# One layer stack on one core: value products paired every eight slots, two copies of x moved in SyncE's queue, eight first max scores moved into the first phase

## The chip, the cores and the metric

The kernel runs on one core of a Trainium2 chip. A core has a matrix engine (TensorE, PE in the rows, with its weight loads as PEld), a vector engine (VectorE, DVE), a scalar engine (ScalarE, ACT), GpSimd (POOL), and SyncE (SP), which here only issues DMAs. The engines have queues of their own, run in the order in which the program was written for each, and meet at semaphores. The metric is the device time of one execution in microseconds (us). The kernel before took 1245.22 us in the median of three runs (1243.57 to 1249.75).

## The reference, cut to what matters

```python
# x: 8 sequences of 512 tokens, 256 wide; 16 heads of 16
def attention_a(x):                       # plain: every query sees every key
    q, k, v = heads(x @ qkv_w.T + qkv_b)
    p = softmax(q @ k.T / sqrt(16))
    return (p @ v) @ out_w.T + out_b
def attention_b(x):                       # causal, with rotary positions
    q, k = rotate(heads(x @ Wq.T)), rotate(heads(x @ Wk.T))
    p = softmax(where(causal, q @ k.T / sqrt(16), -1e9))
    return (p @ v) @ Wo.T
def ffn(x):                               # soft tree of depth 8: 255 gates, 256 leaves
    gate = sigmoid((x @ Wq.T) @ routers.T)
    return (leaf_products(gate) @ leaf_values) @ Wout_w.T + Wout_b
x = x + attention_a(layernorm(x)); x = x + ffn(layernorm(x))
x = x + attention_b(layernorm(x)); x = x + ffn(layernorm(x))
```

## The kernel before

**Phases and slots.** Eight sequences with two attentions each make 16 phases. `causal(n)` says which are causal: phases 3, 5, 7, 9, 11, and 13 to 15. One phase is the attention of one sequence (16 heads, 512 queries, 512 keys), cut into 64 slots. Four slots make a step: a group `g` of four heads against one block `kb` of 128 keys. In a slot TensorE issues:

- one score matmul (line 1068, `ps_max<-k_stack,q_stack`) into one of three PSUM banks `ps_max`. VectorE takes the largest score of each query from it (lines 829 and 825, 825 in a causal phase). This runs `LEAD` = 28 slots ahead, so from slot 36 on it works for the next phase. I call it S below.
- one keyed matmul (line 1090, `ps_key<-q_stack,k_stack`): the same scores with the keys on the rows, already less the largest score, into one of two banks `ps_key`. ScalarE turns it into `probs` (line 737, the exp). I call it K.

**Value products.** `mixed` (line 1114, `ps_out<-probs,v_ones`) multiplies the four `probs` of a step with the values: four matmuls of 32 columns of weights each, side by side in TensorE's four column tiles, all other matmuls of the kernel being one over all 128 columns. In the trace each is two instructions, so a step is a row of x8. `MIX_LAG` = 8 puts step s at slot 4s + 8, so there is one at every slot that is a multiple of four. In a causal phase block kb covers only 512, 384, 256 or 128 queries.

**The largest scores' way.** After 16 score units VectorE turns `neg_max` (line 840), SyncE sends it by four DMAs into a row of `q_stack` (line 471), and the K of that head group waits for them. In the opening 28 units run before slot 0, and the first send follows the unit of slot -10.

**The other work** sits in the same slots by hand-written tables (`FINISH`, `PREPARE_PLAIN`, `PREPARE_CAUSAL`, `LATE`): output projection, layernorm (lines 924 to 954), gates (1197), the tree's levels (976 to 985) and mixing of the phase before, and heads (1222), rotation and the bf16 parts of q and k of the next. For a causal next phase `high_q`, `middle_q` and `low_q` come at slots 20, 22 and 23. SyncE then copies each part into `q_stack` by DMAs (`stack`, line 495): six for the high part, four for the middle one, two for the low one. S at slot 36 is the first to need them all, since it is unit 0 of the next phase.

**Copies of x.** x lives in several tiles; `keep` copies `x_moved` to `x_kept` (line 558), `move` copies `x_plain` to `x_moved` (line 548). `move` waits until the `keep` before it has landed. In phases 4, 6, 8, 10 and 12 both are issued by SyncE with `project_out` 1 of the phase before, at slot 23, and that table entry sorts ahead of `low_q` 1 in the same slot. The line that a sentence can't say is the sum that decides which value products stand in a slot:

```python
if slot % GROUP == MIX_LAG % GROUP:
    step = (slot - MIX_LAG) // GROUP
```

## Time and profile before

| | |
|---|---|
| median of three runs | 1245.22 us (1243.57 to 1249.75) |
| the profiled execution's own time | 1240.59 us |
| its span | 1238.8 us |
| PE / PEld busy | 1113.4 us (90%) / 545.2 us (44%) |
| DVE / ACT / POOL busy | 927.5 us (75%) / 720.7 us (58%) / 302.8 us (24%) |
| opening, up to the first K | 54.7 us |
| a causal phase (5) / a plain one (6) | 65.8 us / 78.0 us |
| after the last K | about 33 us |

A row gives the start, the length, the engine, the line, the operation, output<-inputs, and a count where rows were merged. Idle time ahead of it stands in brackets with what ended it. Matmuls are pipelined: the next one starts before the row of the last has ended, so what one costs is read from start to start.

### The profile page before, as it was taken

How to read it: one execution, taken by the hardware profiler on the slowest of the kernel's cores; microseconds unless marked ns; L12 is line 12 of the kernel's file. 1: busy time of each engine (PE TensorE's matmuls, PEld its weight loads, DVE VectorE, ACT ScalarE, POOL GpSimd, SP SyncE). 2: the span in 40 equal slices, each digit the busy share in tenths (PEclk: the TensorE clock that was granted, in tenths of full speed). 3: DMA queues.
4: the chain of work that ended last, by engine and by line, in shares of the span. 5: the costliest groups of instructions: out<-in, count | busy, mean ns of one | idle time of the engine just before them, and what ended most of it. 6: DMA issues, size and time to landing. Idle time of an engine off the chain costs nothing.

```text
span 1238.8 us, 18868 instructions
## 1 busy us (share of the span) xinstructions
PE 1113.4 (90%) x6160; PEld 545.2 (44%) x6160; DVE 927.5 (75%) x2599; ACT 720.7 (58%) x1457; POOL 302.8 (24%) x324
## 2 busy tenths in 40 slices
PE   5789999879998999989999898989999898887986
PEld 3133443434544554434544354434544444443544
DVE  3768788767878779867889669777888668875834
ACT  3166755557556675657657574656757566554551
POOL 3011101312223031411324022320315125252210
PEclk9599999989999999999999999999999899998988
DMA  7231401122204050230404141041402203011000
GB/s 211 57 96 42 103 18 35 52 69 83 55 18 136 18 120 2 65 106 18 103 1 127 45 97 24 22 133 33 106 1 66 89 18 103 2 49 55 19 3 32
DMA packets 67122, 75.33 MB, mean 61 GB/s; under 512 B 12465, under 2 KB 52817, under 8 KB 67025
## 3 DMA queue, kind: packets, MB, share of 16 engines
q1 hardware_dynamic: 66960, 74.09, 22.3%
q8 instruction: 50, 0.82, 0.3%
q14 instruction: 48, 0.39, 0.1%
q0 software_dynamic: 64, 0.03, 0.0%
HBM read 12.45 MB, written 4.19 MB: 13 GB/s over the span
## 4 chain that ended last, share of the span: by engine, by line
PE 52%; DVE 24%; SPq 6%; DMA 6%; ACT 5%; issue 4%; POOL 2%; DVEq 0%; ACTq 0%; POOLq 0%
PE ps_work L1197 12%; PE ps_out L1114 11%; PE ps_max L1068 9%; PE ps_key L1090 9%; PE ps_work L1222 8%; DVE neg_max L829 6%; SPq L495 4%; DVE ps_max L825 4%; DMA q_stack<-q_part 3%; DVE scratch L982 3%; ACT probs L737 2%; PE ps_work L1168 2%; DVE scratch L954 2%; DVE scratch L985 2%; DMA x_kept<-x_moved 2%
## 5 line engine op out<-in xcount | busy, mean ns | idle before, releaser
L737 ACT ACTIVATE probs<-ps_key 128x512 f32<-128x512 f32 (+3 forms) x1024 | 514.9, 519 | 440.2 <-PE ps_key L1090 436.3
L1068 PE MATMUL ps_max<-k_stack,q_stack 96*128 96x512 bf16 (+3 forms) x1024 | 359.5, 354 | 75.9 <-DMA q_stack<-q_part 44.8
L829 DVE TENSOR_REDUCE neg_max<-ps_max 128x1 bf16<-128x512 f32 x512 | 336.6, 683 | 88.0 <-PE ps_max L1068 86.7
L1090 PE MATMUL ps_key<-q_stack,k_stack 97*128 97x512 bf16 (+3 forms) x1024 | 353.6, 348 | 15.4 <-ACT probs L737 12.7
L825 DVE CUSTOM_DVE_ANT_0 ps_max<-ps_max,mask_b 128x128 f32<-128x128 f32 (+3 forms) x512 | 247.8, 502 | 151.1 <-PE ps_max L1068 149.6
L1068 PEld LDWEIGHTS ps_max<-k_stack,q_stack 96*128 96x128 bf16 x1024 | 99.8, 98 | 348.9 <-DVE neg_max L829 120.1
L1114 PE MATMUL ps_out<-probs,v_ones 128*32 128x512 f32 (+3 forms) x2048 | 238.7, 539 | 0.6 <-POOL probs L642 0.6
L642 POOL TENSOR_SCALAR_AFFINE_SELECT probs<-probs 128x512 f32<-128x512 f32 x128 | 83.0, 648 | 457.6 <-ACT probs L737 457.0
L1090 PEld LDWEIGHTS ps_key<-q_stack,k_stack 97*128 97x128 bf16 x1024 | 101.3, 99 | 136.6 <-ACT probs L737 85.2
L664 POOL TENSOR_TENSOR rstd<-variance,minus_half 128x4 f32<-128x4 f32 (+1 forms) x34 | 33.2, 976 | 235.9 <-DVE variance L937 204.9
L1168 PE MATMUL ps_work<-ident,scratch 128*128 128x128 f32 x384 | 64.2, 293 | 21.6 <-DMA a_v_bias<-in_a_v_bias 9.3
L1197 PE MATMUL ps_work<-gate_w,turned_block 128*128 128x255 f32 x256 | 73.2, 414 | 1.4 <-ACT turned_block L758 1.4
L1114 PEld LDWEIGHTS ps_out<-probs,v_ones 128*32 128x32 f32 x2048 | 40.6, 109 | 74.6 <-issue 66.8
L825 DVE DVE_READ_ACCUMULATOR2_ANT neg_max<- 128x1 bf16 x512 | 73.0, 143 | 0.0
L1168 PEld LDWEIGHTS ps_work<-ident,scratch 128*128 128x128 f32 x384 | 47.4, 149 | 46.6 <-DVE scratch L954 24.1
L1197 PE MATMUL ps_work<-leaf_w,turned_block 128*128 128x256 f32 x256 | 66.3, 383 | 1.4 <-ACT turned_block L758 1.4
L758 ACT ACTIVATE turned_block<-ps_work 128x512 f32<-128x512 f32 x96 | 57.3, 598 | 12.6 <-PE ps_work L1168 12.4
L684 POOL TENSOR_TENSOR scratch<-scratch,cosine 128x512 f32<-128x512 f32 x32 | 43.5, 1358 | 66.8 <-ACT scratch L773 35.7
L1197 PEld LDWEIGHTS ps_work<-gate_w,turned_block 128*128 128x128 f32 x256 | 53.4, 213 | 12.6 <-ACT turned_block L758 2.0
L704 POOL TENSOR_TENSOR k_part<-scratch,k_part 128x512 bf16<-128x512 f32 x32 | 40.3, 1271 | 67.7 <-ACT k_part L795 67.7
L1197 PEld LDWEIGHTS ps_work<-leaf_w,turned_block 128*128 128x128 f32 x256 | 46.0, 190 | 11.6 <-ACT turned_block L758 1.9
L704 POOL TENSOR_TENSOR q_part<-scratch,q_part 128x512 bf16<-128x512 f32 x32 | 38.0, 1191 | 40.5 <-ACT q_part L795 40.4
(83 smaller groups left out, 1201.0 us busy)
## 6 DMA issues: line engine op xcount, KB each, us to landing
k_stack<-k_part SPq DMA_DIRECT2D x48, 256.0 KB
q_stack<-q_part SPq DMA_DIRECT2D x48, 256.0 KB
k_stack<-k_part SPq DMA_DIRECT2D x96, 128.0 KB
q_stack<-q_part SPq DMA_DIRECT2D x96, 128.0 KB
x_in<-in_x SPq DMA_DIRECT2D x8, 512.0 KB, 4.1
q_stack<-shift_rows SPq DMA_DIRECT2D x256, 1.0 KB, 1.7
x_again<-in_x SPq DMA_DIRECT2D x8, 512.0 KB, 4.0
x_moved<-x_plain SPq DMA_DIRECT2D x7, 512.0 KB, 3.5
```

Source lines behind the costliest of these rows:

```text
L642: pool.affine_select(out=tile, in_=tile, compare_op=ALU.is_ge, fill=0.0, base=0, pattern=[[0, GROUP], [1, P]], channel_multiplier=-1)\
L704: pool.tensor_tensor(parts[which][2][:, i, :], rest_of(which, m)[:, i, :], parts[which][1][:, i, :], ALU.subtract).then_inc(on["low"], 1)
L737: act.activation(probs[step % RING][:, j, q0:T], ps_key[slot % 2][:, 0:T - q0], ACT.Exp, scale=SCALE).then_inc(on["exp_done"], 1)
L758: act.activation(dst[:, :, 2 * P * i:2 * P * i + 2 * P], bank[:, :].rearrange("p (k n) -> p k n", k=KC), ACT.Copy).then_inc(on["turned"], 1)
L825: dve.tensor_tensor_reduce(out=src, in0=src, in1=mask_b[:, T - keys:], scale=-1.0, scalar=-MASKED, op0=ALU.add, op1=ALU.min, accum_out=dst)\
L829: dve.tensor_reduce(out=dst, in_=src, axis=AX_X, op=ALU.max, negate=True)\
L1068: pe.matmul(dst[:, 0:keys], q_stack[n % 2][0:SPLIT_ROWS, h, P * qt:P * qt + P], k_stack[n % 2][0:SPLIT_ROWS, h, 0:keys], start=True, stop= ...
L1090: pe.matmul(ps_key[slot % 2][:, 0:T - q0], k_stack[n % 2][0:STACK_ROWS, h, P * kb:P * kb + P], q_stack[n % 2][0:STACK_ROWS, h, q0:T], star ...
L1114: last = pe.matmul(ps_out[COLS * j:COLS * j + COLS, q0:T], v_flat[n % 2][:, at:at + COLS], probs[step % RING][:, j, q0:T], start=(kb == 0) ...
L1168: last = pe.transpose(by_tile(bank)[:, k, P * t:P * t + P], src[:, 2 * i + t, P * k:P * k + P], ident[:, :])
L1197: last = pe.matmul(by_tile(bank)[:, t, 0:width], turned[:, k, tile], weight[:, k, 0:width], start=(k == 0), stop=(k == KC - 1))
L1222: last = pe.matmul(bank[:, :], weight[:, k, P * i:P * i + P], turned_heads[:, k, :], start=(k == 0), stop=(k == KC - 1))
```

## The change

Three things move; none is added or dropped.

1. `mixed` runs for two steps in a row at slots 4, 12, 20, ..., 60, and no more at slots 0, 8, 16, ..., 56. The later step of each pair stands where it stood, the earlier one four slots later than before. Pairs are of steps (14, 15) of the phase before at slot 4, then (0, 1), (2, 3) and so on; 127 pairs in all, and the last two steps stay in the closing.
2. `keep` and `move` leave `project_out` 1 and go to slots 24 and 31 of the same five phases, behind the stack DMAs of `low_q`.
3. The opening runs 20 score units, not 28; in slots 0 to 7 of phase 0 two units run in each slot.

```diff
+CATCH_UP = 8
+KEEP_SLOT, MOVE_SLOT = 24, 31
+def lead_slots(n, slot):
+
+    if n == 0 and slot < CATCH_UP:
+        return 2 * slot - CATCH_UP, 2 * slot - CATCH_UP + 1
+    return slot,
...
+            def core(n, slot):
+                for at in lead_slots(n, slot):
+                    send_shift(n, at)
...
+                if 0 < n < PHASES - AHEAD and causal(n - 1):
+                    if slot == KEEP_SLOT:
+                        keep()
+                    if slot == MOVE_SLOT:
+                        move()
+
             def project_out(m, i, n, bank):
                 count.add("x_ready")
-                if i == 1 and causal(m) and n < PHASES - AHEAD:
-                    keep()
-                    move()
...
             def opening():
-                for slot in range(-LEAD, 0):
+                for slot in range(-LEAD, -CATCH_UP):
                     send_shift(0, slot)
...
             def core(n, slot):
-                largest(n, slot)
+                for at in lead_slots(n, slot):
+                    largest(n, at)
...
             def core(n, slot):
-                ahead(n, slot)
+                for at in lead_slots(n, slot):
+                    ahead(n, at)
                 if out_due(n, slot) is not None:
-                    turn_out(out_due(n, slot), 1, bank_of["turn_out", n, slot])
+                    turn_out(out_due(n, slot), 0, bank_of["turn_out", n, slot])
                 by_key(n, slot)
-                if slot % GROUP == MIX_LAG % GROUP:
-                    step = (slot - MIX_LAG) // GROUP
-                    if step >= 0:
-                        mixed(n, step, MIX_LAG - GROUP + 1)
-                    elif n > 0:
-                        mixed(n - 1, step + STEPS, MIX_LAG - GROUP + 1)
+                if slot % (2 * GROUP) == (MIX_LAG + GROUP) % (2 * GROUP):
+                    step = (slot - MIX_LAG) // GROUP - 1
+                    for late in range(2):
+                        if step >= 0:
+                            mixed(n, step + late, MIX_LAG - GROUP + 1)
+                        elif n > 0:
+                            mixed(n - 1, step + late + STEPS, MIX_LAG - GROUP + 1)
```

TensorE in phase 6, from S of slot 16 to S of slot 21, before. L1068 is S, L1090 is K, L1114 a step's value products (x4 in the program), L1197 a half of the output projection:

```order
L1068 MATMUL ps_max<-k_stack,q_stack 128x512
L1090 MATMUL ps_key<-q_stack,k_stack 128x512
L1114 MATMUL ps_out<-probs,v_ones 32x512 x4
L1068 MATMUL ps_max<-k_stack,q_stack 128x512
L1090 MATMUL ps_key<-q_stack,k_stack 128x512
L1068 MATMUL ps_max<-k_stack,q_stack 128x512
L1090 MATMUL ps_key<-q_stack,k_stack 128x512
L1197 MATMUL ps_work<-b_o,turned_block 128x256 x2
L1068 MATMUL ps_max<-k_stack,q_stack 128x512
L1090 MATMUL ps_key<-q_stack,k_stack 128x512
L1197 MATMUL ps_work<-b_o,turned_block 128x256 x2
```

The same place now, from S of slot 16 to the pair at slot 20 (line numbers are those of the changed kernel):

```order
L1082 MATMUL ps_max<-k_stack,q_stack 128x512
L1104 MATMUL ps_key<-q_stack,k_stack 128x512
L1082 MATMUL ps_max<-k_stack,q_stack 128x512
L1104 MATMUL ps_key<-q_stack,k_stack 128x512
L1082 MATMUL ps_max<-k_stack,q_stack 128x512
L1104 MATMUL ps_key<-q_stack,k_stack 128x512
L1213 MATMUL ps_work<-b_o,turned_block 128x256 x2
L1082 MATMUL ps_max<-k_stack,q_stack 128x512
L1104 MATMUL ps_key<-q_stack,k_stack 128x512
L1213 MATMUL ps_work<-b_o,turned_block 128x256 x2
L1082 MATMUL ps_max<-k_stack,q_stack 128x512
L1104 MATMUL ps_key<-q_stack,k_stack 128x512
```

Between the K of slot 16 and the S of slot 17 nothing stands any more; the four products that stood there are now the first half of `L1128 ... x8` behind K of slot 20.

SyncE's queue in phase 4, slots 20 to 40, before: the high, middle and low parts of q are x6, x4 and x2.

```order
L495 DMA q_stack<-q_part 8x16x512 x6
L471 DMA q_stack<-shift_rows 1x16x32 x4
L495 DMA q_stack<-q_part 8x16x512 x4
L558 DMA x_kept<-x_moved 128x1024
L548 DMA x_moved<-x_plain 128x1024
L495 DMA q_stack<-q_part 8x16x512 x2
L471 DMA q_stack<-shift_rows 1x16x32 x4
```

And now:

```order
L492 DMA q_stack<-q_part 8x16x512 x6
L481 DMA q_stack<-shift_rows 1x16x32 x4
L492 DMA q_stack<-q_part 8x16x512 x6
L555 DMA x_kept<-x_moved 128x1024
L545 DMA x_moved<-x_plain 128x1024
L481 DMA q_stack<-shift_rows 1x16x32 x4
```

The two DMAs of the low part now stand ahead of both copies of x.

VectorE at the end of the opening and in slots 0 to 7 of phase 0, before (L829 the largest score, L840 the turn that the first send waits for, L924 to L954 the layernorm of phase 1):

```order
L829 TENSOR_REDUCE neg_max<-ps_max 128x1 x19
L840 STREAM_TRANSPOSE shift_rows<-neg_max 128x32
L829 TENSOR_REDUCE neg_max<-ps_max 128x1 x10
L924 BN_STATS moments<-x_in 128x6 x2
L829 TENSOR_REDUCE neg_max<-ps_max 128x1
L924 BN_STATS moments<-x_in 128x6 x2
```

And now:

```order
L842 TENSOR_REDUCE neg_max<-ps_max 128x1 x19
L853 STREAM_TRANSPOSE shift_rows<-neg_max 128x32
L842 TENSOR_REDUCE neg_max<-ps_max 128x1 x3
L938 BN_STATS moments<-x_in 128x6 x2
L842 TENSOR_REDUCE neg_max<-ps_max 128x1 x2
L938 BN_STATS moments<-x_in 128x6 x2
```

Seven units that stood ahead of the first BN_STATS now stand behind it.

## Rows read from the trace of the kernel before

**Rows 1.** Busy time: stretch, length, PE, PEld, DVE, ACT, POOL; phases 5 and 6.
```profile
432.80:498.60 65.80, 61.79 (x386) 32.57 (x385) 55.18 (x166) 39.94 (x90) 17.46 (x22) 1.00 0.25 57
498.60:576.60 78.00, 71.92 (x385) 34.28 (x384) 59.95 (x158) 49.88 (x92) 19.80 (x16) 0.98 0.24 69
```

**Rows 2.** Waits of PE, whole span: us in total, times, longest.
```profile
PE ps_max L1068 <- DMA q_stack<-q_part: 44.8, 9, 9.2
```

**Rows 3.** Timeline of PE: S of slot 36, phases 4 and 12.
```profile
401.20 0.23 PE L1068 MATMUL ps_max<-k_stack,q_stack 96*128 96x128 bf16 x1 [3.02 <-DMA q_stack<-q_part]
...
974.83 0.29 PE L1068 MATMUL ps_max<-k_stack,q_stack 96*128 96x128 bf16 x1 [4.47 <-DMA q_stack<-q_part]
```

**Rows 4.** Timelines, phase 6: GpSimd's second low part, SyncE's queue, slots 22 to 36.
```profile
528.53 1.16 POOL L704 TENSOR_TENSOR q_part<-scratch,q_part 128x512 bf16<-128x512 f32 x1 [1.36 <-ACT q_part L795]
...
531.61 2.70 SPq L495 DMA_DIRECT2D q_stack<-q_part  x4
534.47 0.53 SPq L558 DMA_DIRECT2D x_kept<-x_moved  x1
...
540.44 1.37 SPq L495 DMA_DIRECT2D q_stack<-q_part  x2
```

**Rows 5.** Timeline of PE, phase 6, slots 36 to 38: the wait and the work behind it.
```profile
545.04 0.23 PE L1068 MATMUL ps_max<-k_stack,q_stack 96*128 96x128 bf16 x1 [4.52 <-DMA q_stack<-q_part]
...
545.42 1.86 PE L1114 MATMUL ps_out<-probs,v_ones 128*32 128x512 f32 x8
547.21 0.40 PE L1068 MATMUL ps_max<-k_stack,q_stack 96*128 96x256 bf16 x1
...
549.25 0.33 PE L1068 MATMUL ps_max<-k_stack,q_stack 96*128 96x384 bf16 x1
```

**Rows 6.** Timeline of VectorE, phase 12, slot 37.
```profile
978.12 0.75 DVE L924 BATCH_NORM_STATS2 moments<-x_moved 128x6 f32<-128x256 f32 x2
```

**Rows 7.** Timeline of PE: value products of 128 columns (phase 3) and of 512.
```profile
326.37 0.42 PE L1114 MATMUL ps_out<-probs,v_ones 128*32 128x128 f32 x8
326.73 0.39 PE L1068 MATMUL ps_max<-k_stack,q_stack 96*128 96x512 bf16 x1
...
390.02 0.38 PE L1068 MATMUL ps_max<-k_stack,q_stack 96*128 96x512 bf16 x1
390.24 0.38 PE L1090 MATMUL ps_key<-q_stack,k_stack 97*128 97x512 bf16 x1
390.55 1.06 PE L1114 MATMUL ps_out<-probs,v_ones 128*32 128x512 f32 x8
391.55 0.39 PE L1068 MATMUL ps_max<-k_stack,q_stack 96*128 96x512 bf16 x1
```

**Rows 8.** Timelines, phase 6: exp of slot 15 (ACT), K of slot 18.
```profile
518.10 0.58 ACT L737 ACTIVATE probs<-ps_key 128x512 f32<-128x512 f32 x1
...
519.71 0.39 PE L1090 MATMUL ps_key<-q_stack,k_stack 97*128 97x512 bf16 x1 [0.37 <-ACT probs L737]
```

**Rows 9.** Timelines, phase 6: exp of slot 39 (ACT), K of slot 41 (PE).
```profile
551.13 0.60 ACT L737 ACTIVATE probs<-ps_key 128x512 f32<-128x512 f32 x1 [0.22 <-PE ps_key L1090]
...
553.72 0.38 PE L1090 MATMUL ps_key<-q_stack,k_stack 97*128 97x512 bf16 x1
```

**Rows 10.** Timeline of PE, phase 5: S of slot 47, among the tree's levels.
```profile
480.12 0.39 PE L1068 MATMUL ps_max<-k_stack,q_stack 96*128 96x512 bf16 x1 [0.65 <-DVE neg_max L829]
```

**Rows 11.** Timelines of VectorE, SyncE and PE, end of the opening to slot 8.
```profile
50.04 6.02 DVE L829 TENSOR_REDUCE neg_max<-ps_max 128x1 bf16<-128x512 f32 x10
56.79 0.75 DVE L924 BATCH_NORM_STATS2 moments<-x_in 128x6 f32<-128x256 f32 x2 [0.72 <-DMA x_in<-in_x]
...
52.75 0.53 SPq L450 DMA_DIRECT2D x_in<-in_x  x1
...
54.73 0.63 PE L1090 MATMUL ps_key<-q_stack,k_stack 97*128 97x512 bf16 x1
...
64.33 0.38 PE L1068 MATMUL ps_max<-k_stack,q_stack 96*128 96x512 bf16 x1
```

More of the change, by code:

```diff
@@ L472, in send_shift @@
                       .then_inc(sent, DMA)
-            def core(n, slot):
-                send_shift(n, slot)
-                if slot == 0:
-                    if n > 0:
-                        count.add("keyed_full", SLOTS)
-                    else:
-                        load_x(1)
-                if slot == 10 and n + 2 < PHASES and not causal(n + 2):
-                    load_x(n + 2)
-                if slot == 40 and not causal(n):
-                    load_again(n)
             def stack(m, which, part):
@@ L559, in keep @@
                 count.add("kept")
+            def core(n, slot):
+                for at in lead_slots(n, slot):
+                    send_shift(n, at)
+                if slot == 0:
+                    if n > 0:
+                        count.add("keyed_full", SLOTS)
+                    else:
+                        load_x(1)
+                if slot == 10 and n + 2 < PHASES and not causal(n + 2):
+                    load_x(n + 2)
+                if slot == 40 and not causal(n):
+                    load_again(n)
+                if 0 < n < PHASES - AHEAD and causal(n - 1):
[3 more added lines that the diff above has]
+                        move()
             def project_out(m, i, n, bank):
                 count.add("x_ready")
-                if i == 1 and causal(m) and n < PHASES - AHEAD:
-                    keep()
-                    move()
             def mix(m, i, n, bank):
@@ L873, in opening @@
                 dve.tensor_scalar(leaf_w[:, :, :], leaf_w[:, :, :], 2.0 ** -LEVELS, None, ALU.mult).then_inc(folded, 1)
-                for slot in range(-LEAD, 0):
+                for slot in range(-LEAD, -CATCH_UP):
                     largest(0, slot)
@@ L1153, in opening @@
                 pe.wait_ge(ones_set, 2 * DMA)
-                for slot in range(-LEAD, 0):
+                for slot in range(-LEAD, -CATCH_UP):
                     ahead(0, slot)
```

## The prediction, made before the changed kernel was run

> **What bounds the kernel now.** I read the busy time by stretch first, then the waits of TensorE, then the timelines around those waits. In the middle of the kernel TensorE bounds: in phase 5 its rows cover 61.8 of 65.8 us, in phase 6 71.9 of 78.0, while VectorE has 55.2 and 60.0 and ScalarE 39.9 and 49.9 [rows 1]. VectorE is near enough that it takes over for a few slots at a time. The largest wait of TensorE by far is for DMAs into q_stack: 44.8 us in nine times [rows 2]. Five of these nine are the same event, S of slot 36 in phases 4, 6, 8, 10 and 12, with 3.02, 4.52, 4.50, 3.98 and 4.47 us (first and last in [rows 3]), 20.5 us together. In the opening TensorE follows VectorE, which takes one score unit each 0.60 us (10 in 6.02, [rows 11]).
>
> The sum is made against the profiled execution, 1240.6 us (span 1238.8). The median of the runs stands 4.6 us above it; I carry the difference over to the median.
>
> **Part 1, the copies of x.** In phase 6 SyncE issues the four DMAs of the middle part from 531.61, then keep at 534.47; then it sits until that copy has landed, issues move at 539.82 and only at 540.44 the last two DMAs of q [rows 4]. Their issue ends at 541.8, S of slot 36 starts at 545.04 [rows 5], so landing takes 3.9 us from the last issue (the second of two that take 0.69 each, hence 541.1). After the change these two follow the four directly: issue 534.5 to 535.8, landed at about 539.0. GpSimd had made the second half of the low part by 529.7 [rows 4], so they need not wait for it. TensorE reaches S of slot 36 at 545.04 - 4.52 = 540.5, 1.5 us after that landing, so the whole wait goes: 20.5 us in five places. What is late next is at most a VectorE or ScalarE that used the wait to catch up; behind slot 36 the scores are causal and short, so little is queued there.
>
> More goes with it. Behind the wait the rows run at the lower of TensorE's two clocks: value products of 512 columns take 1.79 us from start to start (545.42 to 547.21) against 1.00 elsewhere [rows 5, 7], and the 2.04 us up to 549.25 hold S, K and gates that I put at 1.3 at the full clock. That is 0.8 + 0.7 = 1.5 us in each place, 7.5 us in all. Bounds for this item: 0, if the clock falls there for another reason, and 8.
>
> keep and move themselves now land later. Only phase 12 feels it: there layernorm reads x_moved in slot 37, at 978.12 [rows 6]. With the wait gone that becomes about 972.5; keep issued near 966.4 and move near 971.1, after 4.6 us of landing, would land at 974.6. VectorE would stand for 2 us, and TensorE has three banks to spend meanwhile: cost 1 us, between 0 and 2. Part 1: -20.5 - 7.5 + 1 = **-27 us**, between -18 and -29.
>
> **Part 2, the first max scores.** Without eight of the 28 units the opening looks shorter, but the first K also waits for the send of the largest scores, and the fourth DMA of that send is issued only at about 52.1, just ahead of 52.75, and needs about 1.7 us. So K can start at about 53.9, not 54.73 [rows 11]: 0.8 gained. In exchange VectorE has nothing to do from about 52 on. Its order now has the layernorm's BN_STATS of slot 0 behind the units of slot 0, and x_in lands at 56.79 in either kernel (issue 52.75). Until then VectorE had done the units through slot 0; now it stands in front of that instruction with seven units still to do. 7 x 0.60 = 4.2 us are pushed behind 56.79, into slots where VectorE had no gap: it ran without a pause until the unit of slot 7 at 63.88, and S of slot 8 came at 64.33 [rows 11]. Three banks let TensorE run ahead by up to about 1 us more than before. I take **+3 us**, between +2 (the banks help fully) and +5 (the lower clock, with which this stretch runs, also lasts longer).
>
> **Part 3, the paired value products.** What a pair saves is read from rows of two widths: 128 columns take 0.36 us from start to start, 512 take 1.00 [rows 7]. The difference is 0.64 for 384 columns, 0.213 per 128, so 0.147 of each group is not columns. Ahead of the group K takes 0.31 instead of the 0.22 that S takes (390.24 to 390.55, and 390.02 to 390.24, [rows 7]): 0.09 more. A pair should pay this once, 0.19 to 0.24 us saved: 127 pairs, -24 to -30 us. The rows thus show a cost of going in and out of the column tiles. The Trainium skill says the same (TensorEngine Tiling (Array Packing), Key Properties: changing the tiling mode drains TensorE, changing the tile does not); by that rule alone part 3 would be the whole 24 to 30 us of gain, and that is a rival below.
>
> Against it stands what the groups covered. Call 8j the slot that loses its group. TensorE gets to K and S of the next slots 1.09 us earlier (0.65 where the lost group has 256 columns). But K of slot 8j+1 needs the exp of slot 8j-1, K of 8j+2 the exp of 8j, and the next three S need banks that VectorE frees from work issued before 8j. None of these comes earlier. So TensorE waits anew for 1.09 less the slack that was there, and at 8j+4 it pays the group all the same. A slot with slack gains 0.19; one with none loses 1.09 - 0.24 = 0.85.
>
> I read the slack at the eight places of phases 5 and 6, which later phases repeat. The ends are these. Slot 16 of phase 6 has none: the exp of 15 starts at 518.10, even behind the group, and K of 18 still waits 0.37 us for ScalarE [rows 8]. Slot 40 has much: the exp of 39 is over at 551.73, K of 41 starts at 553.72 [rows 9]. In phase 6 slots 8 and 40 have enough, 0 and 32 a part, 16, 24, 48 and 56 next to none: about 4.9 us of new waits. In phase 5 slots 8, 24 and 40 have enough or nearly, 0 and 56 half, 16, 32 and 48 none, but the groups lost at 16, 32 and 48 are the short ones: about 3.2 us.
>
> Two things give some back. TensorE's other work in slots 8j+1 to 8j+4 also comes earlier and feeds VectorE and ScalarE earlier. The heads at slots 10 and 11 do so for the chain that made slot 16 tight (about 0.6). Slots 41 to 44 do it for the tree's levels: VectorE starts these earlier by up to 1.09, and it is they that hold S of slots 47 to 51 [rows 10] (about 1.1 a phase). So phase 6: 4.9 - 0.6 - 1.1 - 8 x 0.19 = +1.7; phase 5: 3.2 - 0.6 - 1.1 - 1.5 = 0. Mean +0.85, over 15 phases **+13 us**. Both ends: -24 (nothing of the cover was needed) and +45 (nothing is given back, +3 a phase). I take the value near the middle since the rows show both kinds of slot in about equal number.
>
> **Sum:** -27 + 3 + 13 = -11. From 1245.2: **1234 us**; the profiled execution would be near 1230.
>
> **Rivals.**
> - *The pairs are free.* The stretches between groups hold other work of TensorE, and TensorE's own total is what bounds [rows 1]. Then -27 + 3 - 25 = -49: 1196 us. Against it: [rows 8], where the exp is late although a group stood ahead of it.
> - *The pairs starve and stall.* Two banks for the exp and three for the scores cannot bridge a double group and the seven slots of bare S and K behind it. The place is slots 16, 24, 48 and 56; the price 0.85 each, and +3 us a phase or +45 in all; -27 + 3 + 45 = +21: 1266 us. It decides from net new waits of 3.1 us a phase on: 1.6, since parts 1 and 2 give 24 us to 15 phases, and the 1.5 saved. Beside it stands a rule that speaks against this change: the Trainium skill (Perfetto Trace Analysis, Optimization Strategy) advises to interleave stretches with different most-contended engines, and reads a gap that repeats as too few PSUM buffers. The waits of [rows 8, 10] are such gaps.
> - *The DMA wait was cover.* VectorE and ScalarE stand idle for it and start fresh; without it their arrears last into slots 37 to 50, and only about 10 us of part 1 are kept: -10 + 3 + 13 = +6: 1251 us. For it: VectorE is busy through most of slots 14 to 35. Against: the causal scores behind slot 36 are short.
> - *The low part still lands late*, since its two DMAs wait for GpSimd and not for the queue; the time is as in the last case. Against it: 529.7 lies 4.8 us ahead of 534.5 [rows 4].
>
> **How the numbers follow.** Forecast 0.60; pairs free 0.12; pairs starve 0.15; the last two together 0.13. The predicted time is the forecast's, 1234. For a range of eight in ten I leave out the free pairs (0.12) and the worst of the starving ones (0.08): from 1214 (forecast with part 3 at -7) to 1258 (part 3 at +35, or part 1 at -18 with part 3 at +28). About 0.5%, 6 us, is what a measurement of this kernel can tell from no change. Faster by more: 0.50 of the forecast, and the free pairs, 0.62. Within: 0.09 and most of the third case, 0.20. Slower: 0.18.
>
> **What would show it.** In the changed kernel's trace the two low DMAs stand right behind the four, and S of slot 36 in the five phases has no wait for q_stack; the rows behind it are at the full clock. If a wait is left there, part 1 is wrong. A row of value products x16 of 512 columns takes 1.90 us to the next S, not 2.0; if not, the saving is wrong. K of slots 17 and 18 and S of 25 and 49 carry new waits of up to 1 us; TensorE's waits for ScalarE and VectorE grow by about 35 us in all, and those at slots 47 to 51 shrink. If they grow by under 10 us the first rival holds, if by over 60 the second. In phase 0 VectorE stands for over 4 us ahead of the BN_STATS at 56.8, and S of slot 8 comes at about 67.5, not 64.33.

## The result, and the profile after

| | median | lowest to highest | runs |
|---|---|---|---|
| before | 1244.39 us | 1241.38 to 1249.75 | 4 |
| after | 1230.15 us | 1228.47 to 1230.48 | 4 |

The ratio is 0.9878, with a 95% interval of 0.9843 to 0.9914. That is 15 us faster, between 11 and 20. The profiled execution took 1230.48 us, with a span of 1228.8 (1238.8 before). The forecast was 1234 us, and 1230 for the profiled execution. Of all executions below one is in a slow state, the profiled one of `pairs_where_slack` (1288.17 us, granted clock 0.83 where the others have 0.95 to 0.97), and that kernel's median and ratio leave it out.

The page of the changed kernel, busy time by engine, and its row of the granted clock in 40 slices:

```profile
PE 1100.0 (90%) x6160; PEld 563.5 (46%) x6160; DVE 914.6 (74%) x2599; ACT 714.3 (58%) x1457; POOL 302.1 (25%) x324
PEclk9589999979999999999989999899989999997998
```

TensorE is busy 13.4 us less, and the span is 10.0 us shorter. So it is busy for less time and idle for 3.4 us more. The two phases of [rows 1], after (same columns; the stretches are K of slot 0 to the next K of slot 0):

```profile
438.68:507.26 68.58, 63.91 (x387) 34.69 (x385) 55.37 (x166) 39.79 (x91) 17.46 (x22) 0.95 0.24 55
507.26:578.93 71.67, 68.42 (x385) 34.84 (x384) 57.71 (x158) 49.16 (x92) 19.75 (x16) 1.00 0.25 75
```

Phase 6 lost 6.3 us (78.0 to 71.7) and its clock is full now, where it was 0.98. Phase 5 gained 2.8 us (65.8 to 68.6) and its clock fell to 0.95. The waits of TensorE over the whole span (us in total, times, longest):

```profile
PE ps_key L1104 <- ACT probs L750: 34.6, 92, 0.9
PE ps_max L1082 <- DMA q_stack<-q_part: 22.3, 4, 9.2
PE ps_max L1082 <- DVE neg_max L842: 19.7, 32, 2.0
PE ps_max L1082 <- DVE neg_max L838: 9.7, 22, 1.7
PE ps_key L1104 <- DMA q_stack<-shift_rows: 3.1, 1, 3.1
```

The wait for q_part of [rows 2] halved: 44.8 us in nine became 22.3 in four. The first line was 12.7 us in 35 before; the third and fourth were 18.2 and 11.0. The last line is new.

**Slot 36 of phase 6**, as in [rows 4, 5]: first SyncE's queue, then TensorE.

```profile
538.97 4.04 SPq L492 DMA_DIRECT2D q_stack<-q_part  x6
543.17 0.53 SPq L555 DMA_DIRECT2D x_kept<-x_moved  x1
```

```profile
547.97 0.23 PE L1082 MATMUL ps_max<-k_stack,q_stack 96*128 96x128 bf16 x1
...
548.35 1.92 PE L1128 MATMUL ps_out<-probs,v_ones 128*32 128x512 f32 x16
550.21 0.28 PE L1082 MATMUL ps_max<-k_stack,q_stack 96*128 96x256 bf16 x1
...
551.41 0.33 PE L1082 MATMUL ps_max<-k_stack,q_stack 96*128 96x384 bf16 x1
```

All six DMAs of q stand in one row, keep behind them, and S of slot 36 has no bracket. The pair of two groups of 512 columns takes 1.86 us from its start to the next S (548.35 to 550.21). Two single groups take 2.00 by [rows 7], and behind the wait one alone took 1.79 by [rows 5]. From that S to the next one it is 1.20 us (550.21 to 551.41), where [rows 5] had 2.04 (547.21 to 549.25). The same stretch before and after, with the granted clock behind the five engines (0.62, then 1.00):

```profile
545.00:549.50 4.50, 4.46 (x18) 2.03 (x19) 1.46 (x6) 1.68 (x3) 0.00 (x0) 0.62 0.00 0
```

```profile
547.90:551.50 3.60, 3.57 (x26) 1.59 (x26) 1.33 (x6) 1.35 (x3) 0.00 (x0) 1.00 0.39 155
```

**Where the time went.** I cut each profiled execution at its K of slot 0. A row is one execution of one kernel, in us against the first profile of before. The other kernels are explained below; each is one profile, so the table serves for places and not for verdicts.

| | opening | phase 0 | 1 to 3 | 4, 6, 8, 10, 12 | 5, 7, 9, 11 | 13 to the end | span |
|---|---|---|---|---|---|---|---|
| before | 54.7 | 72.2 | 229.4 | 387.3 | 263.3 | 231.9 | 1238.8 |
| before_again | +0.7 | -1.3 | +0.9 | +3.3 | +1.5 | +0.1 | 1243.9 |
| after | -1.1 | +7.7 | +4.1 | -29.0 | +10.8 | -2.4 | 1228.8 |
| moves_only | +1.0 | -1.3 | +1.0 | -29.4 | 0.0 | +0.1 | 1210.1 |
| moves_pairs | -0.4 | +0.9 | +3.8 | -29.5 | +5.0 | -0.1 | 1218.4 |
| pairs_only | +1.1 | +1.4 | +2.3 | +1.3 | +4.4 | -0.8 | 1248.4 |
| first_only | +0.2 | +5.9 | +1.4 | +1.9 | 0.0 | -0.1 | 1248.1 |
| pairs_slack | +1.1 | +1.1 | -1.8 | -35.4 | -2.7 | -1.0 | 1200.2 |
| pairs_tight | -0.3 | -0.3 | +8.2 | -22.8 | +3.9 | +3.2 | 1230.7 |
| pair_40 | 0.0 | 0.0 | -2.8 | -33.7 | -4.0 | -3.1 | 1195.1 |
| slack_24_early | -0.1 | -0.6 | -2.6 | -33.8 | -4.0 | -3.1 | 1194.7 |
| first_early_x | -0.2 | +3.7 | +3.8 | -29.0 | +9.0 | -2.2 | 1223.9 |
| moves_early_x | -0.6 | -1.0 | +2.5 | -29.4 | +2.5 | +1.6 | 1214.4 |

### The profile page after: what moved, and what is told of

It is laid out like the page before. It is cut to its first block, busy times and chain, and to the rows that moved or that the text cites. A ratio compares the mean times of both kernels' runs of the same rounds, so it can differ in the third digit from the quotient of the medians.

```text
span 1228.8 us, 18868 instructions
## 1 busy us (share of the span) xinstructions
PE 1100.0 (90%) x6160; PEld 563.5 (46%) x6160; DVE 914.6 (74%) x2599; ACT 714.3 (58%) x1457; POOL 302.1 (25%) x324
## 4 chain that ended last, share of the span: by engine, by line
PE 56%; DVE 18%; ACT 14%; issue 4%; SPq 4%; DMA 3%; POOL 1%; ACTq 0%; DVEq 0%; POOLq 0%
PE ps_out L1128 13%; PE ps_work L1213 13%; PE ps_key L1104 10%; PE ps_max L1082 9%; PE ps_work L1238 8%; ACT probs L750 7%; DVE neg_max L842 5%; DVE ps_max L838 3%; PE ps_work L1184 3%; SPq L492 2%; ACT turned_block L771 2%; DVE scratch L996 2%; DMA q_stack<-q_part 2%; DVE scratch L999 2%; DVE moments L938 2%
## 5 line engine op out<-in xcount | busy, mean ns | idle before, releaser
L1082 PE MATMUL ps_max<-k_stack,q_stack 96*128 96x512 bf16 (+3 forms) x1024 | 360.0, 357 | 52.5 <-DMA q_stack<-q_part 22.3
L1128 PE MATMUL ps_out<-probs,v_ones 128*32 128x512 f32 (+3 forms) x2048 | 210.9, 531 | 0.6 <-POOL probs L655 0.6
L1128 PEld LDWEIGHTS ps_out<-probs,v_ones 128*32 128x32 f32 x2048 | 54.5, 111 | 104.1 <-issue 88.3
L1184 PEld LDWEIGHTS ps_work<-ident,scratch 128*128 128x128 f32 x384 | 50.6, 154 | 41.4 <-DVE scratch L968 15.2
L1213 PE MATMUL ps_work<-gate_w,turned_block 128*128 128x255 f32 x256 | 67.9, 390 | 1.4 <-ACT turned_block L771 1.4
L1213 PEld LDWEIGHTS ps_work<-gate_w,turned_block 128*128 128x128 f32 x256 | 49.4, 197 | 10.7 <-ACT turned_block L771 1.9
```

The lines of the kernel that those rows point to most:

```text
L1082: pe.matmul(dst[:, 0:keys], q_stack[n % 2][0:SPLIT_ROWS, h, P * qt:P * qt + P], k_stack[n % 2][0:SPLIT_ROWS, h, 0:keys], start=True, stop= ...
L1128: last = pe.matmul(ps_out[COLS * j:COLS * j + COLS, q0:T], v_flat[n % 2][:, at:at + COLS], probs[step % RING][:, j, q0:T], start=(kb == 0) ...
L1184: last = pe.transpose(by_tile(bank)[:, k, P * t:P * t + P], src[:, 2 * i + t, P * k:P * k + P], ident[:, :])
L1213: last = pe.matmul(by_tile(bank)[:, t, 0:width], turned[:, k, tile], weight[:, k, 0:width], start=(k == 0), stop=(k == KC - 1))
```

## The experiments

The theory is the prediction's: part 1 gives about 27 us, part 2 costs about 3, and part 3 costs about 13, because the places differ in slack. The rivals are free pairs, pairs that cost everywhere, and a DMA wait that was cover.

### Each part alone

All diffs are against the changed kernel. The kernels did not all run on the same chip, so differences between two of them go by their ratios to the kernel before, measured beside each, unless medians or spans are named. **moves_only** has part 1 alone. Slots that PAIRED names lose their group, which is then done with the next one, four slots later; here there are none:

```diff
-CATCH_UP = 8
+CATCH_UP = 0
+PAIRED = ()
...
-                    turn_out(out_due(n, slot), 0, bank_of["turn_out", n, slot])
+                    turn_out(out_due(n, slot), 0 if slot - 1 in PAIRED else 1, bank_of["turn_out", n, slot])
...
-                if slot % (2 * GROUP) == (MIX_LAG + GROUP) % (2 * GROUP):
-                    step = (slot - MIX_LAG) // GROUP - 1
-                    for late in range(2):
...
+                if slot % GROUP == 0 and slot not in PAIRED:
+                    step = (slot - MIX_LAG) // GROUP
+                    for at in ((step - 1, step) if slot - GROUP in PAIRED else (step,)):
```

> Only the copies of x are moved (keep at slot 24, move at slot 31); the opening and the single value products are those of the kernel before. My theory: the low part's two DMAs follow the four directly, the waits of S of slot 36 for q_stack (20.5 us in phases 4, 6, 8, 10 and 12) go and the lower clock behind them too, so 27 us less than the kernel before, between 18 and 29: near 1218 us. Rival, the wait was cover: about 10 us less, the rest comes back as waits for VectorE and ScalarE in slots 37 to 50 of the even phases. Rival, the low part lands late anyway: under 5 us less.

Measured: 1215.19 us (1211.83 to 1217.94), ratio 0.974 (0.9704 to 0.9777), 32 us less. In the table the gain is in one column: -29.4 us in the five phases that have the wait, within 1.3 us elsewhere. TensorE around slot 36 of phase 6:

```profile
536.17 0.22 PE L1083 MATMUL ps_max<-k_stack,q_stack 96*128 96x128 bf16 x1
...
536.54 1.06 PE L1129 MATMUL ps_out<-probs,v_ones 128*32 128x512 f32 x8
537.53 0.28 PE L1083 MATMUL ps_max<-k_stack,q_stack 96*128 96x256 bf16 x1
```

The group takes 0.99 us, where [rows 5] had 1.79. K of slot 36 comes 4.7 us earlier in phase 6, counted from its own K of slot 0, K of slot 38 6.3 us earlier, K of slot 48 6.6. So the wait is gone, 1.6 us more is the clock in the two slots behind it, and nothing is given back. Both rivals of part 1 fall.

**pairs_only** has part 3 alone (CATCH_UP = 0, and keep and move in project_out, as before):

```diff
-CATCH_UP = 8
+CATCH_UP = 0
...
-                if 0 < n < PHASES - AHEAD and causal(n - 1):
-                    if slot == KEEP_SLOT:
-                        keep()
-                    if slot == MOVE_SLOT:
-                        move()
...
             def project_out(m, i, n, bank):
                 count.add("x_ready")
+                if i == 1 and causal(m) and n < PHASES - AHEAD:
+                    keep()
+                    move()
```

> Only the value products are paired, at all eight places of a phase; the copies of x and the opening are those of the kernel before. My theory: 13 us more than before, since new waits for the exp and the max outweigh 0.19 to 0.24 us saved in each of 127 pairs. What the trace of the changed kernel suggests: about 2.7 us more in each odd phase from 5 on, and little in the even ones, hence 5 to 15 us more. Rival, the pairs are free: 25 us less. Rival, they starve and stall: 45 us more. A DMA wait in front of slot 36 may hide part of what pairs cost in slots 8 to 35 of the even phases; then this kernel shows less of a loss than the difference of moves_pairs and moves_only does.

Measured: 1251.17 us, ratio 1.003 (1.0008 to 1.0051), 4 us more, where the sum said 13 and the trace of the changed kernel 5 to 15. Pairs are neither free nor ruinous; both were expected to cost more than this.

**first_only** has part 2 alone: PAIRED is empty and keep and move stand in project_out.

```diff
+PAIRED = ()
...
-                if 0 < n < PHASES - AHEAD and causal(n - 1):
-                    if slot == KEEP_SLOT:
-                        keep()
-                    if slot == MOVE_SLOT:
-                        move()
...
             def project_out(m, i, n, bank):
                 count.add("x_ready")
+                if i == 1 and causal(m) and n < PHASES - AHEAD:
+                    keep()
+                    move()
```

> Only the first eight units of max scores are moved from the opening into the slots 0 to 7 of phase 0. Recorded estimate: 3 us more than before, between 2 and 5. By the half phases of the changed kernel's trace it may be 5 to 7 us: the opening ends 1.1 us earlier, phase 0 up to slot 36 is 6.2 us longer. Rival, the opening's VectorE is the bottleneck and eight units less in it are a gain: 3 to 5 us less.

Measured: 1250.13 us, ratio 1.003 (1.0007 to 1.0052), again 4 us more (2 by the medians). So units taken out of the opening are no gain, and that rival falls. The table puts 5.9 us into phase 0 and next to nothing into the opening. The opening did not get shorter although VectorE does eight units less in it.

**moves_pairs** is the changed kernel without part 2:

```diff
-CATCH_UP = 8
+CATCH_UP = 0
```

> The copies of x moved and the value products paired, with the opening of the kernel before. If the three parts add, this is the changed kernel less part 2: 1230 less 3 us by the recorded estimate, near 1227, or 1224 by the half phases of its trace; against moves_only it is the price of the pairs with the DMA wait gone: +13 us by my sum, -25 if pairs are free, +45 if they stall. If this difference is larger than that of pairs_only to the kernel before, the DMA wait was cover for the pairs.

Measured: 1222.60 us (1220.14 to 1226.34), ratio 0.9804 (0.9768 to 0.9839). Against moves_only, on the same chip, the pairs cost 7.4 us by the medians, 8 by the ratios (about 1 to 15). That is more than the 4 us of pairs_only, but it does not show that the DMA wait was cover for them: the intervals overlap, and in the five phases with the wait the pairs cost 1.3 us where it stands and nothing where it is gone (-29.5 against -29.4 in the table). From here to the changed kernel part 2 costs 7.5 us by the medians and 9 by the ratios (about 4 to 14). The three single parts add to -32 + 4 + 4 = -25 us; together they make -15. The intervals of the four ratios together are about 7 us wide to either side, so most of that gap of 10 can be scatter. By places it lies in phases 5 to 11, in the section on the clock below.

### Pairs by place

The prediction sorted the eight places by slack. Two kernels test the sorting. Each is moves_only with one line changed; first pairs_slack, then pairs_tight:

```diff
+PAIRED = (8, 40)
```

```diff
+PAIRED = (16, 24, 48, 56)
```

> The copies of x moved as in moves_only (1215.2 us), and the value products paired only where slots 8 and 40 lose their group, the two places that my prediction found with slack. My theory: each such pair gains 0.19 us and slots 41 to 44 hand the tree its head start (1.1 us a phase), so 6 to 20 us less than moves_only, 1196 to 1209. Rival, read from the starts of K in moves_pairs against moves_only: places 8 and 40 give +0.4 and -0.2 in odd phases, 0 and +0.1 in even ones, so 1 to 3 us more than moves_only. Rival, pairs are free: 6 us less.

> The copies of x moved as in moves_only (1215.2 us), and the value products paired only where slots 16, 24, 48 and 56 lose their group, the places that my prediction found without slack. My theory: up to 0.85 us more for each in even phases and half of that in odd ones, so 20 to 35 us more than moves_only. Rival, read from the starts of K in moves_pairs: +0.6, -0.8, -0.3 and +0.6 in even phases, +0.4, +0.2, -0.3 and +0.1 in odd ones, and 3 us less at the end of phase 15: so within 0 to 5 us more than moves_only. Rival, pairs are free: 12 us less.

Measured: pairs_slack 1201.80 us (1198.31 to 1202.58), ratio 0.9636; pairs_tight 1234.01 us (1232.41 to 1237.75), ratio 0.9906. Against moves_only that is 13 us less and 21 us more by the ratios, each give or take 6. The first is in the middle of the theory's range, the second at its lower end; pairs that are free and pairs that cost everywhere both fall. The two kernels add to +8, which is what all eight pairs cost in moves_pairs. The reading from moves_pairs, in which the places seemed nearly alike, falls too: there every place stands behind another pair, and can take up or hide what that one lost, as slot 24 does below.

Why place 16 costs all, in phase 6. First moves_only, slots 16 to 18, then pairs_tight:

```profile
512.97 0.38 PE L1105 MATMUL ps_key<-q_stack,k_stack 97*128 97x512 bf16 x1
513.28 1.07 PE L1129 MATMUL ps_out<-probs,v_ones 128*32 128x512 f32 x8
514.28 0.39 PE L1083 MATMUL ps_max<-k_stack,q_stack 96*128 96x512 bf16 x1
514.55 0.39 PE L1105 MATMUL ps_key<-q_stack,k_stack 97*128 97x512 bf16 x1
```

```profile
522.05 0.38 PE L1105 MATMUL ps_key<-q_stack,k_stack 97*128 97x512 bf16 x1
523.09 0.39 PE L1083 MATMUL ps_max<-k_stack,q_stack 96*128 96x512 bf16 x1 [0.66 <-DVE neg_max L843]
523.63 0.39 PE L1105 MATMUL ps_key<-q_stack,k_stack 97*128 97x512 bf16 x1 [0.15 <-ACT probs L751]
```

From K of slot 16 to K of slot 17 it is 1.58 us in both (512.97 to 514.55, 522.05 to 523.63). The group of 1.0 us that left has been replaced by waits of 0.66 and 0.15. At slot 20 the group is paid all the same, and K of slot 22 stands 0.9 us later than in moves_only. That is the 0.85 of the prediction.

**pair_40** isolates the best place, with `PAIRED = (40,)`:

> moves_only (1215.2 us, span 1210.1) with one pair per phase, at slot 40. My theory: this place alone carries the gain of pairs_slack, since here TensorE's transposes of slots 41 to 44 and with them VectorE's tree levels come 1.1 us earlier, and it is VectorE that holds S of slots 47 to 51: K of slot 64 comes 0.7 to 1.0 us earlier in each of 15 phases and up to 2 us in the last, so 12 to 14 us less than moves_only, 1198 to 1203. Rival, the saving of each pair (0.2 us) is all there is to it, as at slot 8: 3 us less.

Measured: 1197.26 us (1195.47 to 1198.58), ratio 0.962 (0.9596 to 0.9644), 15 us less than moves_only, a little more than the 12 to 14 expected. One pair a phase gives more than eight. The rival of 3 us falls. Phase 5, slots 40 to 48, VectorE and TensorE of moves_only:

```profile
470.45 0.69 DVE L843 TENSOR_REDUCE neg_max<-ps_max 128x1 bf16<-128x512 f32 x1 [0.64 <-PE ps_max L1083]
...
477.06 0.94 DVE L997 SCALAR_TENSOR_TENSOR scratch<-scratch 128x512 f32<-128x512 f32 x1
```

```profile
468.83 0.27 PE L1105 MATMUL ps_key<-q_stack,k_stack 97*128 97x256 bf16 x1
469.03 1.06 PE L1129 MATMUL ps_out<-probs,v_ones 128*32 128x512 f32 x8
...
475.93 0.39 PE L1083 MATMUL ps_max<-k_stack,q_stack 96*128 96x512 bf16 x1 [0.65 <-DVE neg_max L843]
```

and of pair_40:

```profile
464.59 1.28 DVE L843 TENSOR_REDUCE neg_max<-ps_max 128x1 bf16<-128x512 f32 x2
...
471.51 0.94 DVE L997 SCALAR_TENSOR_TENSOR scratch<-scratch 128x512 f32<-128x512 f32 x1
```

```profile
464.28 0.27 PE L1105 MATMUL ps_key<-q_stack,k_stack 97*128 97x256 bf16 x1
...
470.38 0.39 PE L1083 MATMUL ps_max<-k_stack,q_stack 96*128 96x512 bf16 x1
471.65 0.39 PE L1083 MATMUL ps_max<-k_stack,q_stack 96*128 96x512 bf16 x1 [0.82 <-DVE neg_max L843]
```

Count from K of slot 40, the first TensorE row of each. In moves_only the group holds S of slot 41 back, and VectorE stands 0.64 us for it, at the head of the stretch in which it has the tree to do. In pair_40 that gap is gone (two max scores in one row of 1.28), the tree's last level starts after 7.23 us instead of 8.23, and S of slot 47 after 6.10 instead of 7.10, without its wait. K of slots 48 to 64 stays 1.0 us early. In this stretch VectorE bounds, and the pair gives it work sooner. Phases 6, 8 and 10 gain 0.7, 0.9 and 1.1 us by it.

**pairs_where_slack** and **slack_24_early** put pairs where the single places looked good. The first:

```diff
+def paired(n, slot):
+    if n == PHASES - 1:
+        return slot in (8, 40, 48, 56)
+    return slot == 40 or slot == 8 and n % 2 == 0 and 0 < n < 14
```

> The copies of x moved, the opening of the kernel before, and the pairs only where the slots showed slack: slot 40 in every phase, slot 8 in phases 2, 4, 6, 8, 10 and 12, and slots 8, 40, 48 and 56 of the last phase. Against pairs_slack (1201.8 us, spans 1200.2) this drops the pairs at slot 8 of phases 0 and 14, which cost 0.8 and about 1 to 2 us there, and those of the odd phases (+0.3 each), and adds the two of the last phase (1.4 us less): my theory of slack by place says 4 to 7 us less than pairs_slack, near 1196. Rival, a pair is worth the same wherever it stands: fewer pairs, hence less gain, 3 us more than pairs_slack.

Measured: 1195.84 us, ratio 0.9618 (0.959 to 0.9646). The median is where it was expected; by the ratios it is 2 us less than pairs_slack, give or take 5, so the 4 to 7 us are not shown, and the 3 us more of the rival lie just outside. What refutes equal worth is the 21 us of pairs_tight. Against pair_40 nothing changes: the pairs at slot 8 and those of the last phase bring nothing that can be measured.

The second adds slot 24 and the early load of x, whose edit stands in the next section:

```diff
+    return slot == 40 or slot in (8, 24) and n % 2 == 0 and 0 < n < 14
```

> pairs_where_slack with two edits more: a pair at slot 24 of phases 2, 4, ... 12, and the load of x for phase 1 at the head of SyncE's opening. In pairs_tight the pair at slot 24 of the even phases stood behind one at slot 16 and took back its 0.9 us, down to -0.3. If it does the same alone: 1.2 us less in each of five phases, 6 us less than pairs_where_slack; if it only repaid what slot 16 had lost: within 2 us; if it is a place without slack, as my prediction said (0.85 each): 4 us more. The early load gives up to 0.7 us.

Measured: 1198.55 us, ratio 0.9634 (0.9608 to 0.9659), level with pairs_where_slack within the intervals; the 6 us of gain did not come. From K of slot 0 to K of slot 36 phase 6 takes 42.1 us, 41.8 in moves_only, although the pair at slot 8 alone takes 0.2 off it in pairs_slack. So a pair at slot 24 alone costs 0.5 us. In pairs_tight it repaid what slot 16 had lost (K of slot 22 at +0.9, K of slot 32 at -0.3); it earns nothing by itself.

### The opening

**first_early_x** and **moves_early_x** load x for phase 1 early, in the changed kernel and in moves_only:

```diff
-                    else:
-                        load_x(1)
...
             def opening():
+                load_x(1)
                 for slot in range(-LEAD, -CATCH_UP):
                     send_shift(0, slot)
```

> The changed kernel with one edit: SyncE issues the load of x for phase 1 at the head of its opening, ahead of the first send of largest scores, and no longer in slot 0 behind the second. Theory: what part 2 costs is VectorE's wait for x_in (4.88 us ahead of the first BN_STATS at 56.57), with TensorE held behind it and the lower clock lasting until 70 instead of 64. With x there early the wait goes and S of slot 8 comes at 65 instead of 69.6: 4 to 6 us less than the changed kernel, near 1225. If the cost lies in the seven units themselves and not in the wait, under 2 us less.

> moves_only with the load of x for phase 1 at the head of SyncE's opening. In moves_only VectorE waits under 1 us for x_in, since the eight units stand ahead of it; so 0 to 1 us less than moves_only (1215.2 us), where the same edit took 4.5 us off the changed kernel. If the early load is worth the same here, the wait was not made by part 2.

Measured: first_early_x 1225.67 us (1224.5 to 1226.23), ratio 0.9834 (0.9812 to 0.9856), 4.5 us less than the changed kernel by the medians and 5 by the ratios; moves_early_x 1215.44 (1211.86 to 1218.32), ratio 0.976 (0.9733 to 0.9786), no gain on moves_only. In the table phase 0 is 4.0 us shorter by it with part 2 (+7.7 to +3.7) and not without (-1.3 to -1.0). So the early load repairs something that part 2 broke. It does not repair all: moves_pairs (1222.6) is still 3 us faster by the medians. The rows of the opening in the changed kernel, as in [rows 11], VectorE and then TensorE:

```profile
49.85 1.84 DVE L842 TENSOR_REDUCE neg_max<-ps_max 128x1 bf16<-128x512 f32 x3
56.57 0.75 DVE L938 BATCH_NORM_STATS2 moments<-x_in 128x6 f32<-128x256 f32 x2 [4.88 <-DMA x_in<-in_x]
```

```profile
53.62 0.61 PE L1104 MATMUL ps_key<-q_stack,k_stack 97*128 97x512 bf16 x1 [3.14 <-DMA q_stack<-shift_rows]
...
57.98 0.61 PE L1082 MATMUL ps_max<-k_stack,q_stack 96*128 96x512 bf16 x1 [2.05 <-DVE neg_max L842]
...
60.86 0.61 PE L1082 MATMUL ps_max<-k_stack,q_stack 96*128 96x512 bf16 x1 [1.43 <-DVE neg_max L842]
...
69.56 0.63 PE L1082 MATMUL ps_max<-k_stack,q_stack 96*128 96x512 bf16 x1
```

VectorE makes its three units by 51.7 and stands until 56.57. TensorE waits 3.14 us for the send, so K of slot 0 comes at 53.62. S of slot 8 comes at 69.56, where [rows 11] had 64.33. From K of slot 0 to S of slot 8 TensorE takes 15.9 us instead of 9.6: its waits for VectorE grow from 1.2 to 4.2 us, and seven S more stand in the stretch, at 0.43 us each another 3.0. In first_early_x S of slot 8 comes at 67.9 (65 was expected), and VectorE again stands, now 2.38 us, for a max score whose S cannot be issued because K of slot 0 stands ahead of it on TensorE:

```profile
52.49 0.74 DVE L938 BATCH_NORM_STATS2 moments<-x_in 128x6 f32<-128x256 f32 x2
55.60 1.29 DVE L842 TENSOR_REDUCE neg_max<-ps_max 128x1 bf16<-128x512 f32 x2 [2.38 <-PE ps_max L1082]
```

The lower clock also lasts longer. Stretches of 4 us in before, after and first_early_x (the granted clock stands behind the five engines):

```profile
62.00:66.00 4.00, 4.00 (x22) 2.13 (x21) 3.22 (x7) 2.72 (x5) 0.00 (x0) 0.72 0.01 1
```

```profile
62.00:66.00 4.00, 3.32 (x8) 0.69 (x8) 4.00 (x9) 1.73 (x3) 0.00 (x0) 0.50 0.00 0
66.00:70.00 4.00, 4.00 (x15) 2.51 (x14) 2.86 (x6) 1.65 (x3) 0.00 (x0) 0.50 0.00 0
70.00:74.00 4.00, 3.35 (x10) 1.26 (x9) 2.08 (x3) 2.21 (x5) 0.00 (x0) 0.91 0.28 46
```

```profile
66.00:70.00 4.00, 3.61 (x11) 1.60 (x9) 2.64 (x5) 2.06 (x5) 0.00 (x0) 0.59 0.01 1
```

Before, the granted clock rises from the lower level (1.2 GHz) to the upper one at about 64 us. After, with TensorE waiting up to 66, it rises at about 70.

### The kernel before once more

**before_again** is the kernel before, unchanged.

> The kernel before, unchanged, once more with a profile. Its 19 timed executions of the last call fall into a few at 1240 and most at 1248 us; the execution profiled first had 1240.6. If it lands at 1248, the stretches in which its K of slots 0 and 36 come later than in the first profile show where a single profile of the kernel before may differ by 8 us without any edit: I expect them in the odd or even phases' second half, where the granted clock falls for 1 to 2 us, and 1 us in the opening.

Measured: 1245.99 us (1240.17 to 1252.64); its profile has a span of 1243.9, 5.1 us over the first, not the 8 that I looked for. The places are the expected ones: 0.7 us in the opening, 1.6 behind slot 36 of phase 7, 2.9 behind slot 36 of phases 4, 6, 8, 10 and 12, 1.2 behind slot 36 of phase 2; phase 0 is shorter by 1.3.

## Why the prediction was right, and where it was not

**Part 1, -27 us.** Right in mechanism, place and size. The five phases lost 29.4 us in moves_only; the sum had 20.5 of waits and 7.5 of clock. What was off is the 1 us for x_moved. VectorE does wait for it in phase 12, 0.92 us where 2 were forecast:

```profile
971.74 0.75 DVE L938 BATCH_NORM_STATS2 moments<-x_moved 128x6 f32<-128x256 f32 x2 [0.92 <-DMA x_moved<-x_plain]
```

but TensorE's rows from 967.8 to 972.9 show no wait. The price was 0, the lower bound. By the ratios the part gives 32 us (28 to 37). The sum has no term for the 3 us beyond the profile's column; the scatter of the kernel before is as large.

**Part 2, +3 us.** The mechanism was right, the term mis-sized. VectorE stood 4.88 us ahead of the BN_STATS ("over 4"), K of slot 0 came at 53.62 (53.9 forecast), but S of slot 8 came at 69.56, not 67.5. The step that failed is "Three banks let TensorE run ahead by up to about 1 us more than before". The banks gave nothing of it. I pushed seven units of VectorE behind 56.79 and forgot that TensorE has the same seven S to issue there, 0.43 us each at the lower clock, where they had been in the opening; by 68.10 it is VectorE that waits for one of them, 0.62 us; and I gave the lower clock a part of the 2 us of the upper bound where it stayed 6 us longer. Phase 0 grew 7.7 us in the changed kernel (1 to 1.4 of it in moves_pairs and pairs_only too, without part 2), 5.9 in first_only. By the ratios part 2 costs 4 us alone (1 to 6) and 9 on top of the others (about 4 to 14); the forecast was 2 to 5. By the profiles half of what it costs on top lies outside phase 0, and had no term at all.

**Part 3, +13 us.** The sign and the reason were right, the size somewhat high: 7 to 8 us on top of part 1. The saving is a little over the forecast: 1.86 us for the pair where 1.90 was named. Over all groups the value products take 24 us less from start to start (228.5 to 204.3). About 4 of these are waits and low clock behind single groups; with waits left out, moves_only to moves_pairs, it is 20 (220.5 to 200.2). The K ahead of each of 127 lost groups comes on top: it takes 0.31 us ahead of a group and 0.22 ahead of an S, in moves_only and in moves_pairs (medians), 11 us in all. So by this estimate a pair saves 0.24 us, 31 in all, where the sum took 0.19; and since the pairs cost 8, nearly 39 us of new waits and low clock stand against it. TensorE's waits for ScalarE and VectorE grew from 41.9 to 64.0 us, 22 where 35 was forecast. The rest is in waits too short for a bracket (under 0.15 us) and in low clock; no run divides it. By places:

- Slot 16 costs 0.85 to 0.9 in phase 6, as forecast, and K of slot 17 has a new wait (that of slot 18 keeps its 0.37 us, as in [rows 8]):

```profile
526.92 0.39 PE L1104 MATMUL ps_key<-q_stack,k_stack 97*128 97x512 bf16 x1 [0.78 <-ACT probs L750]
```

- Slot 40 gives 0.2 at once and 0.8 by the tree's head start in phase 5: 1.0, forecast 0.19 + 1.1. S of slot 47 lost the wait of [rows 10], S of slot 49 waits 0.85 us instead of 0.28:

```profile
486.39 0.38 PE L1082 MATMUL ps_max<-k_stack,q_stack 96*128 96x512 bf16 x1
...
489.11 0.39 PE L1082 MATMUL ps_max<-k_stack,q_stack 96*128 96x512 bf16 x1 [0.85 <-DVE neg_max L842]
```

- Slot 8 was put among the places with slack. In phase 6 it gives 0.2; in phase 5, and alike in 7, 9 and 11, it costs 0.3. That was wrong for the odd ones.
- Slot 24: the wait that I named at slot 25 of phase 5 is not there (S of slot 26 has none either, the projection to values behind it 0.18). In phase 6 the place costs 0.5 alone and gives back behind a pair at 16.
- I added the places as if each stood alone. Next to each other they do not add: in phase 6 slot 16 costs 0.9 and slot 24 alone 0.5, and the two together give 0.3. The even phases in moves_pairs thus came to +0.1 (phase 6) where the sum had +1.7, and the odd ones to +1.0 (phase 5) where it had 0: 1.1 a pair of phases, against 1.7. That the total is near is in part luck, since the two kinds of phase are off in opposite directions.

The rule of the Trainium skill (TensorEngine Tiling (Array Packing), Key Properties) that a change of mode drains TensorE agrees with the 0.14 us that one pair saves; taken as the whole story it would have given the first rival, 1196 us, and that was off by 34. The advice of the Trainium skill (Perfetto Trace Analysis, Optimization Strategy) to interleave stretches with different bounds pointed the right way for the places without slack, and the wrong way for slot 40, where the group itself stood in front of the bound engine. Whether more PSUM buffers would close the waits, the other thing that section names, was not tried: no run has a bank more.

**The sum** of -11 us stands against -15 measured (-11 to -20). Its parts were off by -5, +6 and -5, and these partly cancel. The total is better than its terms.

## What to carry to other kernels

A DMA that must wait for another's landing belongs behind those that nobody waits behind: in SyncE's queue, which issues in order, that alone held 32 us here. Before grouping bursts of work on the busiest engine, ask for each place what the others do meanwhile; where they follow, a group that is moved away is replaced by a wait and paid again later, and where such a burst stands in front of another engine's bottleneck, moving that single one is worth more than moving all (15 us of gain against a loss of 7 to 8). Test the places in separate kernels, because neighbours hide each other; and a stretch of prologue that is cut shorter must be looked at for what it waits for next, here a send and a load.

## What the runs showed that I had not expected

**A short fall of the clock behind the same waits, in some phases and not in others.** Slots 52 and 53 of the odd phases (K to K) hold the same work in every phase. In phase 7 of before and of before_again:

```profile
631.15:632.82 1.67, 1.67 (x18) 0.94 (x17) 1.67 (x4) 1.21 (x4) 0.53 (x1) 1.00 0.00 0
```

```profile
632.61:635.61 3.00, 3.00 (x18) 1.51 (x16) 2.20 (x4) 1.73 (x4) 0.53 (x1) 0.51 0.00 0
```

and with a pair in them, phase 5 of moves_pairs and of after:

```profile
487.53:489.63 2.10, 2.10 (x25) 1.20 (x24) 2.10 (x4) 1.82 (x5) 0.64 (x1) 1.00 0.00 0
```

```profile
493.87:497.57 3.70, 3.70 (x25) 1.86 (x24) 1.95 (x4) 2.12 (x5) 0.64 (x1) 0.53 0.00 0
```

TensorE is busy throughout, at the full clock or at the lower one; ahead of it lie slots 45 to 51, in which it waits for VectorE in all of them. A fall costs 1.3 us without a pair and 1.6 with one. Of the five odd phases 3 to 11 it struck none in before, moves_only, first_only, pairs_slack, slack_24_early and pair_40, one in before_again and pairs_tight, two in part in moves_pairs and pairs_only, two in moves_early_x (2.40 and 3.02 us), which has neither a pair nor part 2, and four in after and in first_early_x, the two kernels with all three parts. Over these five the stretch takes 16.6 us in after and 11.2 in moves_pairs: 5.4 of the 10.4 us between their spans. Of part 2's price on top of the others, half is thus not in phase 0, which part 2 touches, but in phases 5 to 11, which it only shifts in time. Apart from the kernel before each has one profile, so this half may be the luck of the profiled execution; the medians (7.5 us apart) do not decide it. Why the clock falls in one phase and not in the other was not tried, and stays open; so does whether this is the reason why three parts together lose more than one by one. It is also one source of the 1240 to 1250 us over which the kernel before scatters.

**The last phases scatter too.** 13 to the end lies between -3.1 and +3.2 us in kernels whose edits there are one or four pairs, and +1.6 in moves_early_x, which has no edit there. A difference of that size in one profile of that stretch says nothing of an edit.
